# Batch 0 of a Strassen-style attention kernel: x in four loads, a new order of its pieces, and the Wv pieces moved

## The reference, cut to what matters

```python
q = jnp.einsum('bnd,ed->bne', x, Wq)
k = jnp.einsum('bnd,ed->bne', x, Wk)
v = jnp.einsum('bnd,ed->bne', x, Wv)
rel = adj.T[None] * jnp.einsum('bnd,bmd->bnm', q, k)
rel = rel / jnp.linalg.norm(rel, axis=2, keepdims=True)
out = layernorm(x + jnp.einsum('bnm,bmd->bnd', rel, v))
```

## Time and profile before

| | |
|---|---|
| median of 3 runs | 1971.75 us (1971.14 to 1971.92) |
| the profiled execution | 1971.97 us, its span 1970.2 us |
| busy: PE, DVE, POOL, ACT | 1957.0, 1531.9, 957.8, 762.5 us |
| granted TensorE clock, mean | 0.997 |
| batch 0 / batch 1, start to start | 129.9 us / 121.0 us |

### The profile page before, as it was taken

The page is one execution under the profiler, slowest core; times in us unless marked ns, Lnnn a source line. Parts: engine busy times, 40 slices in busy tenths (PEclk is TensorE's granted clock), DMA queues, the critical chain, the costliest instruction groups (busy, mean ns, idle before and its releaser), DMA issues.

```text
span 1970.2 us, 28685 instructions
## 1 busy us (share of the span) xinstructions
PE 1957.0 (99%) x9857; PEld 1669.1 (85%) x9857; DVE 1531.9 (78%) x2085; ACT 762.5 (39%) x1288; POOL 957.8 (49%) x639
## 2 busy tenths in 40 slices
PE   8999999999999999999999999999999999999998
PEld 6888888888888888888888888888888888888887
DVE  8796877868778696787968779687796877868775
ACT  5433434335342352423424234342433424335341
POOL 5744536455354553446435374453644536455352
PEclk9999999999999999999999999999999999999999
DMA  5734343344524345343444333443434343344401
GB/s 188 314 134 165 144 167 115 144 154 154 186 92 149 142 157 184 122 151 118 157 175 160 128 139 133 172 153 128 160 128 170 144 155 127 144 154 152 185 26 64
DMA packets 80416, 292.22 MB, mean 148 GB/s; under 512 B 7441, under 2 KB 7441, under 8 KB 76305
## 3 DMA queue, kind: packets, MB, share of 16 engines
q1 hardware_dynamic: 80400, 292.06, 40.2%
HBM read 251.13 MB, written 40.89 MB: 148 GB/s over the span
## 4 chain that ended last, share of the span: by engine, by line
PE 97%; DVE 1%; POOL 1%; DMA 0%; issue 0%; SPq 0%; ACT 0%; POOLq 0%; DVEq 0%
PE banks L422 32%; PE banks L424 32%; PE banks L423 32%; DMA scr<-xT 0%; DVE aw L794 0%; DVE x_lo L755 0%; POOL scr L1063 0%; DVE yv L816 0%; POOL square_sum L1067 0%; POOL squares L1067 0%; SPq L344 0%; POOL scr L1072 0%; SPq L343 0%; POOL res L1075 0%; POOL res L1080 0%
## 5 line engine op out<-in xcount | busy, mean ns | idle before, releaser
L422 PE MATMUL banks<-yv 128*128 128x512 f32 x1024 | 399.8, 390 | 0.0
L424 PE MATMUL banks<-yv 128*128 128x512 f32 x1024 | 398.5, 389 | 0.0
L423 PE MATMUL banks<-yv 128*128 128x512 f32 x1024 | 398.5, 389 | 0.0
L1119 POOL TENSOR_TENSOR square_sum<-square_sum,squares 128x512 f32<-128x512 f32 x224 | 319.9, 1428 | 85.7 <-ACT squares L657 75.1
L422 PE MATMUL banks<-yv,x_hi 128*128 128x512 f32 x896 | 348.7, 389 | 0.5 <-DVE rel L857 0.5
L424 PE MATMUL banks<-yv,x_lo 128*128 128x512 f32 x896 | 348.6, 389 | 0.0
L423 PE MATMUL banks<-yv,x_hi 128*128 128x512 f32 x896 | 348.6, 389 | 0.0
L1136 POOL TENSOR_TENSOR rstd<-var_eps,minus_half 128x1 f32<-128x1 f32 x128 | 144.2, 1127 | 329.3 <-DVE var_eps L968 329.3
L423 PE MATMUL banks<-aw,x_hi 128*128 128x256 f32 x896 | 253.6, 283 | 0.0
L424 PE MATMUL banks<-aw,x_lo 128*128 128x256 f32 x896 | 253.5, 283 | 0.0
L422 PE MATMUL banks<-aw,x_hi 128*128 128x256 f32 x896 | 253.5, 283 | 0.0
(11 more groups left out here) (108 smaller groups left out, 3430.5 us busy)
## 6 DMA issues: line engine op xcount, KB each, us to landing
scr<-adj SPq DMA_DIRECT2D x128, 512.0 KB, 5.8
aw<-w_kept SPq DMA_DIRECT2D x16, 3584.0 KB, 11.1
aw<-a_kept SPq DMA_DIRECT2D x15, 3584.0 KB, 11.0
scr<-xT SPq DMA_DIRECT2D x32, 1024.0 KB, 7.1
res<-x SPq DMA_DIRECT2D x128, 256.0 KB, 2.7
out<-res SPq DMA_DIRECT2D x128, 256.0 KB, 2.0
a_kept<-aw SPq DMA_DIRECT2D x1, 3584.0 KB, 18.2
w_kept<-v_raw SPq DMA_DIRECT2D x3, 512.0 KB, 8.5
```

Source lines behind the costliest of these rows:

```text
L422: pe.matmul(bank_ap, l_hi, r_hi, start=first and i == 0, stop=False, skip_group_check=on)
L423: pe.matmul(bank_ap, l_hi, r_lo, start=False, stop=False, skip_group_check=on)
L424: mm = pe.matmul(bank_ap, l_lo, r_hi, start=False, stop=i == len(pairs) - 1, skip_group_check=on)
L1119: pool.tensor_tensor(square_sum[:, h, :], square_sum[:, h, :], squares[:, n % SQRING, :], ALU.add).then_inc(square_added, 1)
```

## The change

1. `X_PIECES` becomes X11, X22, S1, X12, S2, S3, S4 (it was X22, X11, S1, X12, S3, S2, S4), and the steady batches follow: X11 before X22, S2 before S3 in `X_IN_TILE` and in POOL's sums.
2. Batch 0 loads x in four blocks of 512 KB, in the order X11, X21, X22, X12, each with its own semaphore. S1 and S2 of batch 0 get places of their own in `rel`; S1 is summed on POOL instead of DVE.
3. The lists of ACT, DVE and POOL for batch 0 are rewritten. S3, S4, B22, T3 and T4 move behind the first rounds; T3's lo half goes to POOL. The weight product takes its matmuls in another order (hi*hi first, banks 4 and 5 finished first); the six filling products after it are gone.
4. Wv is split on ACT and DVE during the S stage, straight into `aw`, once `a_kept` is stored. POOL keeps only its four sums. The seven small stores and the reload of `w_kept` in batch 0 are replaced by one store of all of `aw` to `w_kept`.
5. adj tile 2 is loaded early, with tile 3.

The core of the diff:

```diff
-X_PIECES = (X22, X11, S1, X12, S3, S2, S4)
-X_SUMS = (S1, S3, S2, S4)
+X_PIECES = (X11, X22, S1, X12, S2, S3, S4)
+X_SUMS = (S1, S2, S3, S4)
...
-        X_IN_TILE = {0: (X22, X11), 1: (S1,), 2: (X12,), 3: (S3,), 4: (S2,), 5: (S4,)}
+        X_IN_TILE = {0: (X11, X22), 1: (S1,), 2: (X12,), 3: (S2,), 4: (S3,), 5: (S4,)}
+
+
+        first_raw_of = dict(raw_of)
+        first_raw_of.update({S1: rel[:, 2:4, BANK:N], S2: rel[:, HT:HT + 2, 0:BANK]})
...
-        A_PIECES = (B11, T1, B21, T2, T4, T3, B22)
-        A_SUMS = (T1, T3, T2, T4)
-        A_HI = (B11, B21, B22, T1, T2, T4, T3)
+
+        A_PIECES = (B11, T1, B21, T2, T4, B22)
+        A_SUMS = (T1, T2, T3, T4)
+        A_HI = (B11, T1, B21, B22, T2, T4, T3)
...
+            def load_first_x():
+                for n, d in ((0, 0), (1, 0), (1, 1), (0, 1)):
+                    rows = slice(n * BANK, (n + 1) * BANK)
+                    sp.dma_start(raw_block(n, d), xT_v[0, :, 2 * d:2 * d + 2, rows]).then_inc(x_first_loaded[n][d], DMA)
...
-            load_x(0)
+            load_first_x()
             for h in range(2):
                 sp.dma_start(wv_raw[:, 2 * h:2 * h + 2, :], w_v(wvT)[:, 2 * h:2 * h + 2, :]).then_inc(wv_loaded, DMA)
+            load_adj(2)
             load_adj(3)
-
-            def store_wv(i):
-                sp.wait_ge(wv_split, i + 1)
-                sp.dma_start(w_kept_v[:, WV_PIECES[i], :, :], wv_slot[i % WSLOTS]).then_inc(w_stored[i % WSLOTS], DMA)
-
-            for i in range(3):
-                store_wv(i)
...
-                    for i in range(3, 7):
-                        store_wv(i)
-                    load_adj(2)
-                    sp.wait_ge(a_split, 7)
+                    sp.wait_ge(a_split, len(A_PIECES))
+                    sp.wait_ge(a_t3_split, 1)
                     sp.dma_start(a_kept, aw[:, :].bitcast(F32)).then_inc(a_stored, DMA)
+
+                    sp.wait_ge(w_loaded, DMA)
+                    sp.dma_start(w_kept, aw[:, :].bitcast(F32)).then_inc(w_stored, DMA)
                     for t in range(RRING):
                         load_res(0, t)
-                    for i in range(WSLOTS):
-                        sp.wait_ge(w_stored[i], 2 * DMA if i < 3 else DMA)
-                    sp.wait_ge(a_stored, DMA)
-
-                sp.wait_ge(y_done, b * Y_COUNT + Y_COUNT)
-                sp.dma_start(aw[:, :].bitcast(F32), w_kept).then_inc(w_loaded, DMA)
+                else:
+
+                    sp.wait_ge(y_done, b * Y_COUNT + Y_COUNT)
+                    sp.dma_start(aw[:, :].bitcast(F32), w_kept).then_inc(w_loaded, DMA)
...
+            for ks, js in (((0, 1), range(KD)), ((2, 3), (0, 1)), ((2, 3), (2, 3))):
+                for k in ks:
+                    pe.wait_ge(w_hi_made, 2 * k + 2)
+                    for j in js:
+                        pe.matmul(bank[A_BANK + j], wq_hi[:, k, cols(j)], wk_hi[:, k, :], start=(k == 0), stop=False,
+                                  skip_group_check=True)
+                    pe.wait_ge(w_split, 2 * k + 1)
+                    for j in js:
+                        pe.matmul(bank[A_BANK + j], wq_lo[:, k, cols(j)], wk_hi[:, k, :], start=False, stop=False,
+                                  skip_group_check=True)
+                    pe.wait_ge(w_split, 2 * k + 2)
+                    for j in js:
+                        mm = pe.matmul(bank[A_BANK + j], wq_hi[:, k, cols(j)], wk_lo[:, k, :], start=False,
+                                       stop=(k == KD - 1), skip_group_check=True)
+                        if k == KD - 1:
+                            mm.then_inc(a_done, 1)
...
+                act.wait_ge(a_stored, DMA)
+                act.wait_ge(y_done, Y_COUNT)
+                act.activation(wv_hi[:, q, :, :], wv_raw_of[q], ACT.Copy).then_inc(wv_hi_made, 1)
...
-            for q in (X22, X11, S1):
-                x_piece(0, q, True)
+            x_piece(0, X11, True)
             a_hi_piece(B11)
             act.activation(a12_raw, a_block(0, 1), ACT.Copy).then_inc(a12_copied, 1)
-            for q in (B21, B22, T1):
+            x_piece(0, X22, True)
+            a_hi_piece(T1)
+            x_piece(0, S1, True)
+            x_piece(0, X12, True)
+            for q in (B21, B22):
...
-                    for i in range(3, 7):
-                        wv_hi_piece(i)
+                    a_hi_piece(T4)
+                    a_hi_piece(T3)
+                    x_piece(b, S3, True)
+                    x_piece(b, S4, True)
...
+                for name, i in square_order[0:4]:
+                    square(b, name, i)
                 if first:
-
-                    for i in range(WSLOTS):
-                        act.wait_ge(w_stored[i], 2 * DMA if i < 3 else DMA)
-                for name, i in square_order[0:6]:
+                    for i in range(7):
+                        wv_hi_piece(i)
+                for name, i in square_order[4:6]:
...
-            x_piece(0, X22)
-            x_first_sum(S1)
-            x_piece(0, X11)
-            x_piece(0, S1)
+            x_piece(0, X11, True)
             a_lo_piece(B11)
             a_sum_of(T1)
+            x_piece(0, X22, True)
             a_lo_piece(T1)
+            x_piece(0, S1, True)
+            dve.wait_ge(first_sum[S1], 1)
+            dve.tensor_tensor(first_raw_of[S2], first_raw_of[S1], raw_of[X11],
+                              ALU.subtract).then_inc(first_sum[S2], 1)
+            x_piece(0, X12, True)
+            a_lo_piece(B21)
+            a_sum_of(T2)
+            x_piece(0, S2, True)
+            a_lo_piece(T2)
             a_sum_of(T3)
-            a_sum_of(T2)
-            a_lo_piece(B21)
-            x_piece(0, X12)
-            x_first_sum(S2)
-            a_lo_piece(T2)
-            x_piece(0, S3)
-            x_piece(0, S2)
             a_sum_of(T4)
+
+            def wv_lo_piece(i):
+                q = WV_PIECES[i]
+                dve.wait_ge(wv_hi_made, i + 1)
+                lo = dve.tensor_tensor(wv_lo[:, q, :, :], wv_raw_of[q], wv_hi[:, q, :, :].bitcast(F32), ALU.subtract)
+                if i == 6:
+
+                    lo.then_inc(w_loaded, DMA)
...
                 if first:
-                    x_piece(0, S4)
+                    x_piece(b, S3, True)
+                    for j in range(2):
+                        y_lo_piece(b, B11, j, a[j])
+                    x_piece(b, S4, True)
+                    a_lo_piece(B22)
+
+                    dve.wait_ge(a_split, len(A_PIECES))
+                    dve.wait_ge(a_t3_split, 1)
...
+                if first and pair == 1:
+                    wv_lo_piece(4)
+                    wv_lo_piece(5)
...
+                if first and pair == 1:
+                    wv_lo_piece(6)
...
+                if first and pair == 0:
+                    wv_lo_piece(0)
+                    wv_lo_piece(1)
...
+                if first and pair == 0:
+                    wv_lo_piece(2)
+                    wv_lo_piece(3)
...
+            for d in range(2):
+                pool.wait_ge(x_first_loaded[1][d], DMA)
+            pool.tensor_tensor(first_raw_of[S1], x21_raw, raw_of[X22], ALU.add).then_inc(first_sum[S1], 1)
             pool.wait_ge(first_sum[S1], 1)
-            pool.wait_ge(x_loaded[0], DMA)
-            pool.wait_ge(a_split, 1)
+            pool.wait_ge(a_split, a_place[T2])
+            pool.wait_ge(x_first_loaded[0][0], DMA)
             pool.tensor_tensor(raw_of[S3], raw_of[X11], x21_raw, ALU.subtract).then_inc(first_sum[S3], 1)
+            pool.wait_ge(a_hi_made, a_hi_place[T3])
+            pool.tensor_tensor(a_lo[:, T3, :, :], a_raw_of[T3], a_hi[:, T3, :, :].bitcast(F32),
+                               ALU.subtract).then_inc(a_t3_split, 1)
             pool.wait_ge(first_sum[S2], 1)
-            pool.wait_ge(x_split, x_place[X12])
-            pool.tensor_tensor(raw_of[S4], raw_of[X12], raw_of[S2], ALU.subtract).then_inc(first_sum[S4], 1)
-
-            def wv_lo_piece(i):
-                pool.wait_ge(wv_hi_made, i + 1)
-                pool.tensor_tensor(wv_part(i, 1).bitcast(F32R), wv_raw_of[WV_PIECES[i]], wv_part(i, 0),
-                                   ALU.subtract).then_inc(wv_split, 1)
-
-            for i in range(3):
-                wv_lo_piece(i)
-            pool.tensor_tensor(wv_raw_of[T1], wv_block(0, 1), wv_block(0, 0), ALU.subtract).then_inc(wv_sum, 1)
-
-            pool.wait_ge(wv_sum, 1)
-            pool.tensor_tensor(wv_raw_of[T3], wv_block(1, 1), wv_block(0, 1), ALU.subtract).then_inc(wv_sum, 1)
-            pool.tensor_tensor(wv_raw_of[T2], wv_block(1, 1), wv_raw_of[T1], ALU.subtract).then_inc(wv_sum, 1)
-            pool.wait_ge(wv_sum, 3)
-            pool.wait_ge(wv_split, 2)
-
-            pool.tensor_tensor(wv_raw_of[T4], wv_block(1, 0), wv_raw_of[T2], ALU.subtract).then_inc(wv_sum, 1)
-            for i in range(3, 7):
-                wv_lo_piece(i)
+            pool.tensor_tensor(raw_of[S4], raw_of[X12], first_raw_of[S2], ALU.subtract).then_inc(first_sum[S4], 1)
...
```

(45 more changed lines are left out.)

64 lines of the change are left out of this document (29 added, 35 removed).

## The result

The changed kernel takes **1980.05 us** (median of 6 runs, 1979.38 to 1981.19), the kernel before 1971.84 beside it (1971.14 to 1972.31). The ratio is 1.0042, interval 1.0031 to 1.0053: slower by 8.2 us, where 8.0 were forecast.

A forecast was written before the change was run, and what follows sets the result against it. Matmul spacing (TensorE 99% busy) was taken to bound every batch but batch 0, which loses 8.9 us. Start -7.9, Wv +0.9, stall +12.3, clock +2.7 gave +8.0: profiled 1980.0, forecast median 1979.8 us, range 1971.5 to 1986.

The forecast's parts named there:

- Y starts at 16.4: Start of batch 0: the first Y round begins at 16.4 us instead of 19.21.
- A hole of 2.4 us before round 3: Y of batch 0: S4, late as POOL and DVE take turns, leaves TensorE idle for 2.4 us.
- No fall of the clock after it: Y of batch 0, after the small hole: clock taken not to fall, 0 us, upper bound 2.9.
- Part 2: S stage of batch 0: Wv pieces moved to ACT and DVE delay DVE's masks and sums, costing 0.9 us.
- Part 3: SP's queue in batch 0: adj(6), behind w_kept store and res loads, lands 14.8 us after piece 6, at 86.8.
- Stall 12.3: V of batch 0: TensorE waits 12.3 us before the third round, from 84.0 to v_copy at 96.3.
- The clock behind it 2.7: V of batch 0, after the long wait: the lower clock costs 2.7 us, less some slack included.
- Outputs at 113.5: Output stage of batch 0: starts at 113.5 us, given as a sign that the forecast is right.
- Rival 1: SP's queue: adj loads don't wait for the store; faster, -3.5 or -7.5 us (1964.5); chance 0.09.
- Rival 2: No measurable change: piece 6 at 68.0, adj at 82, V stalls 7.4 us; 1974 (1971 with clock up); chance 0.14.
- Rival 3: Slower still: clock also falls after the small hole (+2.9, 1982.7), less kind POOL and DVE turns (+2, 1985); chance 0.22.
- The bound that the prediction gave for every case: V of batch 0: chain from piece 6 to v_copy needs 23.7 us against TensorE's 19.4, so at least 4.3 stall.

The follow-up runs named there:

- e4: e1 with x of batch 0 in two loads of 1 MB, the half with X21 and X22 first, instead of four blocks; 1967.01 us.
- e2: Changed kernel with the four res loads issued behind adj(6) and adj(7), the w_kept store still ahead of them; 1978.02 us.
- e3: e1 with POOL summing S4 before it makes T3's lo half; 1965.36 us.
- e1: Changed kernel with the w_kept store and the res loads moved behind adj(7) in SP's queue; 1965.34 us.
- e5: Changed kernel with adj(6) and adj(7) of the first batch issued from ACT's own DMA queue, at the time of the w_kept store; 1978.18 us.
- e7: e1 with POOL summing S3 first, into a buffer of its own, and S4 right after T2's split; 1964.68 us.
- e8: e7 with DVE's Wv pieces 0 to 3 moved from pair 0 of S into pair 1; 1965.32 us.
- e9: e7 with S3 summed on DVE, between the lo halves of X11 and B11, and POOL starting with S1; 1963.52 us.

## Why the prediction was right, step by step

The time was right within 0.3 us, by the mechanism it named; part of that closeness is luck, since several terms were off and offset each other. The ledger of the profiled run, in its steps:

- **Y starts at 16.4: 17.44.** Sized too early by 1.0. The matmuls ahead of Y kept a spacing of 0.43 us until 6.9 in this profile, and until about 4.3 in before's. Over the nine profiles with the new order the start lies between 16.32 and 18.09 (16.32 to 17.44 without e4). The step had taken one profile's start for the kernel's.
- **A hole of 2.4 us before round 3, S4 late by POOL's turn: shown**, 2.0 over the spacing (34.19 to 36.42). POOL's sums before it:

```profile
25.62 2.41 POOL L1096 TENSOR_TENSOR scr<-scr 128x1024 f32<-128x1024 f32 x1 [9.06 <-issue]
28.65 1.31 POOL L1098 TENSOR_TENSOR aw<-rel,aw 128x512 fp32r<-128x512 f32 x1 [0.63 <-ACT aw L606]
29.90 3.46 POOL L1101 TENSOR_TENSOR scr<-scr,rel 128x1024 f32<-128x1024 f32 x1
```

- **No fall of the clock after it (0, bound 2.9): wrong.** It was 0.50 from 38 to 40 and the round with T2 started at 43.58 instead of 41.7. But the fall cost less than the bound. DVE's sum for that round was ready only at about 42.4, so some 1.1 us are the clock's. In e2 and e3, where it stayed up behind a hole of the same size, that round started at 42.00 and 42.06, after a wait for DVE. In e1, where the clock fell, it started at 43.30; yet of the 1.2 us that e3 was ahead there, 0.2 were left at the outputs (99.00 against 99.24). In both stretches behind it, pair 1 of S and V, e3 took longer, which points to DVE's queue as the bound.
- **Part 2 costs 0.9: 0 here, hidden because TensorE came late.** TensorE, late by the clock, came after DVE, and pair 1 of S took 19.04 us (59.90 to 78.94), as before the change (66.17 to 85.21). In e2, which had kept the clock, it took 19.61:

```profile
58.48 0.39 PE L422 MATMUL banks<-yv,x_hi 128*128 128x512 f32 x1
...
78.09 0.28 PE L422 MATMUL banks<-aw,x_hi 128*128 128x256 f32 x1
```

  So DVE's late list costs about 0.6 us when TensorE comes on time. The Wv pieces did end when forecast: 72.45 against 72.0.
- **Part 3, the landing 14.8 us behind piece 6: 16.4** (72.45 to 88.9), mis-sized by 1.6. Of these, 0.7 were a choice: its nearest row, 12.8 us, and 2.7 for the 1.05 MB more give 15.5. The rest lies in the single rate that it used. The DMA engines in the changed kernel (columns as in the earlier trace rows, the last is GB/s):

```profile
73.00:81.00 8.00, 8.00 (x45) 6.95 (x45) 3.22 (x6) 0.00 (x0) 1.89 (x2) 1.00 1.16 456
81.00:82.00 1.00, 1.00 (x11) 1.00 (x10) 0.00 (x0) 0.00 (x0) 0.00 (x0) 1.00 0.10 29
82.00:83.00 1.00, 1.00 (x10) 1.00 (x10) 0.00 (x0) 0.00 (x0) 0.00 (x0) 1.00 0.39 129
83.00:88.00 5.00, 1.85 (x16) 1.65 (x14) 0.00 (x0) 0.00 (x0) 0.00 (x0) 1.00 1.00 389
```

  The store ran at 0.46 MB per us, then almost nothing moved for 1.5 us (27 GB/s from 81.0 to 82.5), then the loads ran at 0.39. The sum had no such pause between a store and the loads behind it; why it is there stays open. SP's own issuing isn't the cause: the adj loads had been issued by 79.8, before the store was through. e1 and e2 show that the transfers ahead make the delay, e5 that another queue gains only the `res` loads' share.
- **From the landing to `v_copy` 9.5: 9.3** (88.85 to 98.13). **Stall 12.3: 13.5** (84.7 to 98.18, 13.33 as a wait).
- **The clock behind it 2.7: about 2.0.** From 98.18 the outputs are reached in 16.56 us (114.74) against 14.6 at full clock. The fall was read right, but 4.5 us at half speed came out of it, not 5.8, so the term was mis-sized.
- **Outputs at 113.5: 114.74.** `v_copy` is 1.8 late (0.45 from piece 6, 1.6 from the landing, less 0.2), and the clock gave 0.7 back. The 1.0 of the start reaches the outputs only through piece 6, since TensorE then waits anyway. For the same reason the round with T2, 1.9 late, and part 2's missing 0.9 couldn't show in the time: it was right because `v_copy` and the clock behind it set the outputs, and their errors (+1.8 and -0.7) partly cancel. The medians lie 1.0 closer than the profiles, since the profiled run was the slowest of the six.

Rival 1 (the adj loads don't wait for the store) is refuted by e2 and e5. Rival 2 (a stall of 7.4) needed piece 6 at 68.0 and a landing at 82, and had neither. Rival 3's first half, the clock falling after the small hole, happened; its price of 2.9 did not. The bound that the prediction gave for every case, a chain from piece 6 to `v_copy` that is longer than TensorE's work beside it, held in each run that kept adj behind piece 6 (waits of 13.3, 11.0 and 11.0 us in the changed kernel, e2 and e5). But the 19.4 us of work are a slip: the prediction's own times, 74.60 and 91.0, leave 16.4, and the changed kernel had 16.6 (68.06 to 84.7). So its least stall should have been 7.3 us, not 4.3. Only taking adj out of that chain (e1) made the change pay.

The misses of the expectations have something in common. e3, e7 and e8 moved an operation whose wait was seen, and the next wait stood right behind it: in e3 and e7 with POOL and DVE in turns (2.82 and 2.73 us for operations of 0.69 and 1.22), in e8 in V instead of S. e9 took the hole out of Y because it put the sum where DVE had nothing to do and took it from POOL; its gain in time over e7 is within the noise.

## What to carry to other kernels

When a store or load of some MB moves, write down what stands behind it in the queue and when that is wanted: a load that the next masks need goes ahead of a store that nobody waits for. A second queue was no way around here. Read what a late load delays down to the engine that sets the end, and subtract the slack there (1.8 us here). An operation of POOL's that is moved is priced together with the DVE operations it will meet.

## What the runs showed of the hardware

- A load of 0.5 MB needs 3.8 us alone (e1), 13.8 behind a 3.67 MB store in SP's queue (e2), and 14.5 when it is issued beside that store in ACT's queue (e5).
- Two queues took turns packet by packet, 128 to 112 in 10 us, but with packets of 28 KB and 4 KB: the queue with the large packets moved 3.67 MB, the other 0.46 (e5).
- Between the last bytes of that store and the first of the loads behind it almost nothing moved for 1.5 us (27 GB/s from 81.0 to 82.5 in the changed kernel).
- After a wait of 1.8 to 1.9 us the granted clock fell in e1, e4, e5 and the changed kernel, and stayed at 1.00 in e2 and e3. The length of the wait didn't decide it; what did stays open.
- At the start the table gives a granted clock of 1.00 while matmuls of 512 columns follow each other at 0.43 us, the spacing of the lower level, twice the 0.2265 of the upper. The spacing is to be trusted there. It changed at about 4.3 us in the profile of before and at about 6.9 in the changed kernel's, which alone moves the start of Y.
- POOL and DVE in turns: the Trainium skill, SBUF — State Buffer, "SBUF: two separate sides", says that of a GpSimd operation and a DVE operation with two inputs in SBUF the one that starts first holds the port pair they share for its whole instruction. The traces agree: 2.82 us for a DVE operation of 0.69 that met a POOL sum of 2.38.
